# Building a stacked factor operand on chip from eight loaded copies, in a batched low-rank-updated linear layer

## The reference

```python
# x: (32, 512, 512)   fside -> u = v: (32, 1, 512, 16)   cond: (32, 512)   W: (512, 512)   fc_bias: (512,)
z1 = einsum('bfi,bir->bfr', x, v[:, 0]) / 512
z  = einsum('bfr,bor->bfo', z1, u[:, 0]) / 16
y  = einsum('bfi,oi->bfo', x, W) + fc_bias + z + cond[:, None, :]
out = x + gelu(y)                      # exact gelu, float32 throughout
```

## Time and profile before

| | |
|---|---|
| median of three runs | 387.24 us |
| the profiled execution's own time | 387.57 us |
| span of its instructions | 385.8 us (1.8 us lie around it) |
| TensorE (PE) busy | 376.9 us |
| VectorE (DVE) busy | 296.7 us |
| ScalarE (ACT) busy | 204.6 us |
| DMA | 85.75 MB, mean 222 GB/s |

### The profile page before, as it was taken

The page is one execution under the profiler, slowest core; times in us unless marked ns, Lnnn a source line. Parts: engine busy times, 40 slices in busy tenths (PEclk is TensorE's granted clock), DMA queues, the critical chain, the costliest instruction groups (busy, mean ns, idle before and its releaser), DMA issues.

```text
span 385.8 us, 7835 instructions
## 1 busy us (share of the span) xinstructions
PE 376.9 (98%) x3065; PEld 313.8 (81%) x3065; DVE 296.7 (77%) x188; ACT 204.6 (53%) x214; POOL 0.7 (0%) x5
## 2 busy tenths in 40 slices
PE   8998899999999999999999999999999999999995
PEld 3676788888888888888888888888888888888884
DVE  2579967788877878888777897778888787788832
ACT  3467364545566445566545556654465664455531
POOL 0000000000000000000000000000000000000000
PEclk9999899999999999999999999999999999999999
DMA  7879789887777877777787777687767779774222
GB/s 193 229 152 304 220 268 270 265 263 233 213 231 225 261 221 248 211 218 234 239 244 231 244 212 221 213 266 220 256 230 206 230 218 270 216 255 131 110 109 110
DMA packets 27756, 85.75 MB, mean 222 GB/s; under 512 B 6832, under 2 KB 6960, under 8 KB 23776
## 3 DMA queue, kind: packets, MB, share of 16 engines
q1 hardware_dynamic: 27088, 84.41, 71.8%
q10 hardware_dynamic: 656, 1.18, 1.0%
HBM read 35.75 MB, written 33.55 MB: 180 GB/s over the span
## 4 chain that ended last, share of the span: by engine, by line
PE 89%; SPq 5%; DMA 2%; ACTq 1%; ACT 1%; DVE 1%; issue 0%
PE y L420 82%; SPq L178 5%; PE update L489 3%; DMA f_stack<-f_parts 2%; ACTq L274 1%; PE y L404 1%; PE y L412 1%; PE y L408 1%; ACT L279 0%; SPq L164 0%; SPq L192 0%; ACT result L270 0%; DVE result L356 0%; DVE x_low L313 0%; DVE f_parts L313 0%
## 5 line engine op out<-in xcount | busy, mean ns | idle before, releaser
L420 PE MATMUL y<-x_low,w_high 64*128 64x512 f32 x928 | 184.5, 388 | 0.0
L420 PE MATMUL y<-x_high,w_high 64*128 64x512 f32 x928 | 184.5, 388 | 0.0
L270 ACT ACTIVATE result<-y,bias 128x512 f32<-128x512 f32 x128 | 81.4, 685 | 156.9 <-PE y L420 148.6
L420 PE MATMUL y<-x_high,w_low 64*128 64x512 f32 x928 | 125.2, 387 | 0.0
L356 DVE TENSOR_TENSOR result<-result,x_in 128x1024 f32<-128x1024 f32 (+1 forms) x65 | 78.3, 1205 | 56.5 <-ACT result L270 56.5
L420 PEld LDWEIGHTS y<-x_high,w_low 64*128 64x128 f32 x928 | 90.5, 185 | 15.3
L420 PEld LDWEIGHTS y<-x_low,w_high 64*128 64x128 f32 x928 | 90.5, 185 | 15.3
L420 PEld LDWEIGHTS y<-x_high,w_high 64*128 64x128 f32 x928 | 90.3, 185 | 15.3
L317 DVE SCALAR_TENSOR_TENSOR full_w<-update,base_w 128x2048 f32<-128x2048 f32 (+1 forms) x38 | 74.3, 1954 | 23.6 <-PE update L489 16.9
L313 DVE TENSOR_TENSOR x_low<-x_in,x_high 128x2048 fp32r<-128x2048 f32 (+1 forms) x38 | 74.0, 1947 | 5.6 <-ACT x_high L256 5.6
L313 DVE TENSOR_TENSOR w_low<-full_w,w_high 128x2048 fp32r<-128x2048 f32 (+1 forms) x38 | 74.0, 1948 | 0.4
(11 more groups left out here) (15 smaller groups left out, 29.7 us busy)
## 6 DMA issues: line engine op xcount, KB each, us to landing
out_t<-result SPq DMA_DIRECT2D x63, 512.0 KB, 3.1
x_in<-x_t SPq DMA_DIRECT2D x31, 1024.0 KB, 6.5
f_stack<-f_parts SPq DMA_DIRECT2D x186, 64.0 KB, 4.1
f_stack<-f_parts SPq DMA_DIRECT2D x124, 32.0 KB, 3.8
x_in<-x_t ACTq DMA_DIRECT2D x4, 256.0 KB, 9.3
base_w<-w_t SPq DMA_DIRECT2D x4, 256.0 KB, 8.2
f_parts<-factors SPq DMA_DIRECT2D x1, 896.0 KB, 6.8
out_t<-result SPq DMA_DIRECT2D x2, 256.0 KB, 2.5
```

Of the source, the lines that this page charges most:

```text
L270: nc.scalar.activation(result[j % SLOTS][:, m, :], y[m][:, :], ACT.Gelu, bias=bias[:, bass.ds(b * CHUNKS + m, 1)]).then_inc(gelu_ready, 1)
L420: return nc.tensor.matmul(y[m][:, :], w[rows, c, m * P:(m + 1) * P], x[rows, c, :], start=first, stop=last)
```

## The change

The stack is no longer copied together. Each batch's raw factors (16 rows) are loaded from HBM in eight copies into the 128 partitions of `f_raw` by one DMA. ScalarE rounds all 128 rows to `f_high`; VectorE makes each side of the stack as `f_high * low_rows[side] + f_raw`, where `low_rows` is a column with -1 in rows that shall hold the low part and 0 elsewhere. A row with 0 holds the raw factor, which is rounded as it is written in fp32r. The column is made once from row numbers: an iota on GpSimd, two `bitwise_and` and two multiplications on VectorE. `f_raw` has four buffers, `f_high` and `f_stack` two.

`f_first` becomes 128 rows: 16 of factors, 16 of zeros from HBM, 96 zeroed by two VectorE memsets. ScalarE's queue no longer loads factors. SP's first loads come in another order. All four first updates stand ahead of piece 0, and the update of batch 1 moves from ahead of piece 2 to ahead of piece 3, with a wait per chunk. `w_t` and `factors` have other layouts in HBM.

```diff
-    RANK = factors.shape[0] // UNROLL
+    RANK = factors.shape[1]
+    COPIES = P // RANK
-        f_first = sb("f_first", [RANK, FEATURES], fp32)
-        f_parts = sb("f_parts", [UNROLL * RANK, GROUPS, 3, FEATURES], fp32)
+        f_first = sb("f_first", [P, FEATURES], fp32)
+        f_raw = [sb(f"f_raw{s}", [P, FEATURES], fp32) for s in range(UNROLL)]
+        f_high = [sb(f"f_high{s}", [P, FEATURES], fp32r) for s in range(SLOTS)]
...
+        def stacked_in(t, j):
+            return t + (j + 2) // UNROLL, (j + 2) % UNROLL
+        def has_stack(t, j):
+            return not (isinstance(t, int) and t == GROUPS - 1 and j >= UNROLL - 2)
...
         @block.sync
+            def load_factors(t, j):
+                sp.dma_start(f_raw[j][:, :],
+                             factors[bass.ds(UNROLL * t + j, 1)].to_broadcast([COPIES, RANK, FEATURES])
+                             ).then_inc(f_loaded[j], 16)
-            sp.dma_start(f_first[:, :], factors[0:RANK, 0, :]).then_inc(f_first_loaded, 16)
+            sp.dma_start(f_first[0:FIRST_ROWS, :], first_factors).then_inc(f_first_loaded, 16)
             for c in range(CHUNKS):
-                sp.dma_start(base_w[:, c, :], w_t[:, c, :]).then_inc(w_loaded[c], 16)
+                sp.dma_start(base_w[:, c, :], w_t[c]).then_inc(w_loaded[c], 16)
+                if c == 1:
+                    load_factors(0, 1)
             load_x(0, 1)
             sp.dma_start(cond_sb[:, :, :], cond).then_inc(bias_loaded, 16)
             sp.dma_start(fc_sb[:, :], fc_bias).then_inc(bias_loaded, 16)
-            sp.wait_ge(f_low_ready, 1)
-            stack_factors(0, 1)
-            stack_factors(0, 2)
-            sp.dma_start(f_parts[:, 1:GROUPS, 2, :], factors[:, 1:GROUPS, :]).then_inc(f_loaded[1], 16)
-            for j in range(2, X_SLOTS):
-                load_x(0, j)
+            load_factors(0, 2)
+            load_x(0, 2)
+            load_factors(0, 3)
+            load_x(0, 3)
             def step(t, j):
-                if not (last_group and j >= UNROLL - 3):
-                    sp.wait_ge(update_ready, made(b + 1))
-                    stack_factors(t3, j3)
...
                     load_x(t + 1, j)
+                    if not is_first(t, j):
+                        sp.wait_ge(stack_ready, 2 * b)
+                    load_factors(t + 1, j)
...
         @block.scalar
+            def high_factors(t, j):
+                act.wait_ge(f_loaded[j], 16 * (t + 1) if j else 16 * t)
+                if not (isinstance(t, int) and b < SLOTS + 1):
+                    act.wait_ge(stack_ready, 2 * (b - SLOTS))
+                nc.scalar.activation(f_high[j % SLOTS][:, :], f_raw[j][:, :], ACT.Copy).then_inc(f_high_ready, 1)
             for c in range(CHUNKS):
                 high_pieces(0, c)
-                if c == 0:
-                    split_factors(0)
+                if c == 1:
+                    high_factors(0, 1)
             def step(t, j):
...
                     split_x(tn, jn)
                     split_w(tn, jn)
+                    if not piecewise(t, j) and has_stack(t, j):
+                        high_factors(*stacked_in(t, j))
                 for m in range(CHUNKS if is_whole(t, j) else TILES):
                     gelu(t, j, m)
                 if piecewise(tn, jn):
                     for c in range(CHUNKS // 2, CHUNKS):
                         high_pieces(b + 1, c)
-                if j == 0 and not last_group:
-                    split_factors(t + 1)
+                if piecewise(t, j):
+                    high_factors(*stacked_in(t, j))
...
         @block.vector
+            def stack_factors(t, j):
+                if isinstance(t, int) and b == 1:
+                    dve.wait_ge(low_rows_ready, 2)
+                dve.wait_ge(f_high_ready, b)
+                if not (isinstance(t, int) and b < SLOTS + 1):
+                    dve.wait_ge(update_ready, made(b - SLOTS))
+                for side in range(2):
+                    nc.vector.scalar_tensor_tensor(f_stack[slot][:, side, :], f_high[slot][:, :].bitcast(fp32),
+                                                   low_rows[:, side:side + 1], f_raw[j][:, :], ALU.mult,
+                                                   ALU.add).then_inc(stack_ready, 1)
+            nc.vector.memset(f_first[FIRST_ROWS:2 * FIRST_ROWS, :], 0.0).then_inc(f_first_zeroed, 1)
+            nc.vector.memset(f_first[2 * FIRST_ROWS:P, :], 0.0).then_inc(f_first_zeroed, 1)
+            dve.wait_ge(rows_numbered, 1)
+            bits = (2 * RANK, RANK)
+            for side in range(2):
+                nc.vector.tensor_scalar(row_bit[:, side:side + 1], rows[:, :], bits[side], None,
+                                        ALU.bitwise_and).then_inc(bits_ready, 1)
+            dve.wait_ge(bits_ready, 2)
+            for side in range(2):
+                nc.vector.tensor_scalar(low_rows[:, side:side + 1], row_bit[:, side:side + 1], -1.0 / bits[side], None,
+                                        ALU.mult).then_inc(low_rows_ready, 1)
             for c in range(CHUNKS):
                 pieces(0, c)
-                if c == 0:
-                    low_factors(0)
+                if c == 1:
+                    stack_factors(0, 1)
...
-                if j == 1 and not (isinstance(t, int) and t == GROUPS - 1):
-                    low_factors(t + 1)
             def step(t, j):
...
                     low_part(w_low[slot][:, :, :], full_w[:, :, :], w_high[slot][:, :, :], w_low_ready)
+                if has_stack(t, j):
+                    stack_factors(*stacked_in(t, j))
                 if piecewise(t, j):
                     finish_previous(t, j)
                 add_x(t, j, slice(0, HALF))
...
         @block.gpsimd
             nc.gpsimd.memset(idle[:, :], 0.0).then_inc(idle_zeroed, 1)
+            nc.gpsimd.iota(rows[:, :], [[0, 1]], base=0, channel_multiplier=1).then_inc(rows_numbered, 1)
...
         @block.tensor
-                pe.wait_ge(stacked[slot], 16 * STACK_DMAS * uses)
-                pe.wait_ge(full_w_ready, made(b - 1))
+                pe.wait_ge(stack_ready, 2 * b)
+                if not piecewise(t, j):
+                    pe.wait_ge(full_w_ready, made(b - 1))
                 for c in range(CHUNKS):
+                    if piecewise(t, j):
+                        pe.wait_ge(full_w_ready, made(b - 2) + c + 1)
...
+            pe.wait_ge(f_first_zeroed, 2)
             pe.wait_ge(f_first_loaded, 16)
-            for c in range(CHUNKS - 1):
+            for c in range(CHUNKS):
                 first_update(c)
             for c in range(CHUNKS):
-                if c == 1:
-                    first_update(CHUNKS - 1)
-                if c == CHUNKS // 2:
+                if c == CHUNKS - 1:
                     rank_update(0, 1)
                 piece(0, c)
```

More of the change, by code:

```diff
@@ L28, with cond_residual_kernel @@
 UNROLL = 4
-def cond_residual_kernel(nc, x_t, w_t, factors, cond, fc_bias, out_t):
+def cond_residual_kernel(nc, x_t, w_t, first_factors, factors, cond, fc_bias, out_t):
     fp32 = mybir.dt.float32
     fp32r = mybir.dt.float32r
+    int32 = mybir.dt.int32
     ALU = mybir.AluOpType
@@ L39, in cond_residual_kernel @@
     GROUPS = BATCHES // UNROLL
-    RANK = factors.shape[0] // UNROLL
+    RANK = factors.shape[1]
+    FIRST_ROWS = first_factors.shape[0]
+    COPIES = P // RANK
     UPDATE_SCALE = 1.0 / (FEATURES * RANK)
@@ L45, in cond_residual_kernel @@
     TILE = P // TILES
-    STACK_DMAS = 5 * TILES
     HALF = CHUNKS // 2
@@ L90, in cond_residual_kernel @@
         f_first_loaded = sem("f_first_loaded")
-        f_loaded = [sem("f_loaded_group0"), sem("f_loaded_rest")]
+        f_first_zeroed = sem("f_first_zeroed")
+        f_loaded = [sem(f"f_loaded{s}") for s in range(UNROLL)]
+        rows_numbered = sem("rows_numbered")
+        bits_ready = sem("bits_ready")
+        low_rows_ready = sem("low_rows_ready")
         bias_loaded = sem("bias_loaded")
@@ L96, in cond_residual_kernel @@
         f_high_ready = sem("f_high_ready")
-        f_low_ready = sem("f_low_ready")
-        stacked = [sem(f"stacked{s}") for s in range(SLOTS)]
+        stack_ready = sem("stack_ready")
         bias_ready = sem("bias_ready")
@@ L556 @@
     x_t = np.ascontiguousarray(x.transpose(0, 2, 1))
-    w_t = np.ascontiguousarray(np.asarray(L0_cond_W).reshape(P, chunks, P, chunks).transpose(2, 3, 1, 0)
-                               .reshape(P, chunks, features))
-    factors = np.asarray(fside_Bx1x1024x16_0).reshape(batches // UNROLL, UNROLL, P, chunks, rank)
-    factors = np.ascontiguousarray(factors.transpose(1, 4, 0, 3, 2).reshape(UNROLL * rank, batches // UNROLL, features))
+    w_t = np.ascontiguousarray(np.asarray(L0_cond_W).reshape(P, chunks, P, chunks).transpose(3, 2, 1, 0)
+                               .reshape(chunks, P, features))
+    factors = np.asarray(fside_Bx1x1024x16_0).reshape(batches, P, chunks, rank)
+    factors = np.ascontiguousarray(factors.transpose(0, 3, 2, 1).reshape(batches, rank, features))
```

(2 more changed lines are left out.)

33 lines of the change are left out of this document (7 added, 26 removed).

## The result

**Slower by 0.42%.** The changed kernel takes 387.62 us (386.42 to 389.23, 20 runs), the kernel before in the same session 385.87 us (384.55 to 388.07, 20 runs). The ratio is 1.0042, its 95% interval 1.0022 to 1.0061: slower, clear of noise, though the interval's lower end is under the 0.3% that I had taken as the least that can be told. I had forecast 385.9 and given 0.12 to slower. That 387.62 lies inside my range (383.8 to 387.8) is luck: the range reached so far up for a late load at batch 1, which did not come. Note that the kernel before, too, did not come out at the 387.24 of the three runs that I had; that turns out to be part of the error.

The account below looks back on a forecast made before the run. TensorE's back-to-back products bound the kernel, so only the head could gain: -1.4 us from 387.57 gave 386.2, or 385.8 beside the median 387.24; stated 385.9 us. Range 383.8 to 387.8.

Parts of the forecast that it names:

- a late load at batch 1: Batch 1's eight-copy factors landing late; the range's upper end, 387.8 us, assumed landing at 13.6 us with a clock fall.
- the walk through the head: From first updates to batch 3's update, operation times added in the new order: that update at 38.2 us, 1.4 us gained.
- the signs that I had named for being wrong: ScalarE awaiting f_raw past 13 us, VectorE starting past 6.5, batch period above 11.33, or a third TensorE wait in the head.
- the rival: Batch 1's eight-copy load uses only some DMA engines, lands at 12.4 to 15 us: 386.5 to 389.1 us; chance 0.14.
- From batch 3 on the pace is 11.33 in both.: Steady state from batch 3: each batch takes 11.33 us before and after the change, so nothing gained or lost.
- whether VectorE's load fits: Steady state: two added stack operations, 1.37 us, bring VectorE to 10.4 us of each 11.33 us batch, costing nothing.
- Update 3 starts at 38.2 in place of 39.64: 1.4 us gained: Head: batch 3's update, released by VectorE's stack instead of a transfer, starts 1.4 us earlier, at 38.2 us.
- The sum: Whole kernel: head gain of 1.4 us, the clock's fall costing 1.65 us both before and after, steady pace unchanged.
- Its loads wait for a stack made two batches earlier: nothing.: Steady state, SP's queue: factor loads wait only for a stack made two batches earlier, so they cost nothing.
- The stall leaves the clock alone: Rival at the wait before batch 3's update: no clock fall, gain 1.4 + 1.65 = 3.05 us, 384.2 us; chance 0.27.

Follow-up runs that it names:

- second profile of the kernel before: The kernel before, unedited, run and profiled again: 385.27 us, ratio 0.9987; the clock did not fall in this profile.
- the filled wait with the loads first: Changed kernel with small tiles declared last, eight-copy loads at the start of SP's step, and 14 zero products before batch 3's update: 385.28 us, ratio 0.9981.
- second profile of the changed kernel: The changed kernel, unedited, run and profiled again: 387.59 us, ratio 1.0046 to the kernel before.
- the kernel with the wait filled: Changed kernel with 14 products of zeros on TensorE ahead of batch 3's update, nothing else: 387.27 us, ratio 1.0029 to the kernel before.

## Why the prediction was wrong, point by point

**Right: the walk through the head.** The factors of batch 1 are rounded at 11.20 (I had 11.7), update 1 is at 17.71 (17.7), gelu is the next thing late (0.89 at 22.31), update 2 at 29.12 (28.8), the wait ahead of update 3 is 3.15 us (3.3) and ends at 38.68 (38.2), the clock falls again and costs again 12.54 - 10.90 = 1.64 (1.65). The iota takes 0.13 us at 1.29. VectorE has 10.38 us a batch (10.4). That last one is right with one size off: a stack operation takes 747 ns and not 0.69 us.

Of the signs that I had named for being wrong one came, and it is the first failed step below: a batch period above 11.33.

**The load of eight copies.** At 210 us, when the packets on their way are those of the factors' load (98 packets, 0.20 MB in that microsecond, 2 KB each), the DMA share is 0.51 and 195 GB/s move; at 205 us it is 1.03 and 410. Half of the engines' time, then, and half of the rate, as in the rival. The rule of the Trainium skill, DMA: Bandwidth & Descriptors, Rules for kernel authors, agrees with this trace. But ScalarE had the first load at 11.20 us, after 0.46 us of waiting for it and 0.5 before my 11.7, so the rival's cost for batch 1 was not there. It came back in a place that I didn't look at, the factors of batch 4.

**The failed steps** are four.

1. *"From batch 3 on the pace is 11.33 in both."* It is 11.367: 0.033 x 27 = 0.90 us. I had asked for this step whether VectorE's load fits, and it does; with half of it gone the pace stays. The cost came in with three declarations. Shown from both sides: the small tiles moved last take it away, an unused tile of the same size puts 0.027 of it into the kernel before. Against the execution of the earlier trace rows this alone turns 0.93 us of gain into nothing, hence the equal spans.

2. *"Update 3 starts at 38.2 in place of 39.64: 1.4 us gained."* The head gained 0.93 us against that execution, as stack 3 came 0.5 us later than in the walk (its rounding 0.3 late, the two stack operations 1.41 in place of 1.3). That is the mis-sized term. Worse is the base: 39.64 is update 3 in one execution. In the second profile of the kernel before it is at 38.79, and with the unused tiles at 38.35 to 39.67. The term of 1.4 us is 0.1 against the second profile, and 39.64 is near the late end of all six.

3. *The sum was made against an execution of the less frequent kind, and the clock's fall cancelled in it.* I set one fall against one fall. But 38 of 103 runs of the kernel before have a mean clock of 0.996 or less, and 23 of 32 of the changed kernel. That a fall costs 1.6 us where the stack comes no earlier is shown by the filled wait with the loads first. That the longer wait is why it comes more often is supported by the profiles kept. The clock fell behind waits of TensorE for a stack of 1.92, 2.21, 2.24, 2.93, 3.12 (twice), 3.15 and 3.17 us; it stayed up behind all thirteen of 0.41 to 1.61 us, and behind one of 2.93 us, in the second profile of the changed kernel. The wait ahead of update 3 is 1.16 to 2.24 us in the six executions with the head of the kernel before, by how late the stack's transfers land, and 2.93 to 3.17 in the five with the head of the changed one that don't fill it. The frequencies themselves are of runs without a trace, so their cause is not shown run by run. The wait of 0.9 us for gelu, which only the changed kernel has, brings the clock down now and then: in two of the ten profiles that have it.

4. *"Its loads wait for a stack made two batches earlier: nothing."* The load of batch 4 waits for more than that: it stands in SP's queue behind a store and a load of x, issued at 40.65, and ScalarE stands 3.8 us for it. Where the clock falls at update 3 the slow piece covers it; where it doesn't, TensorE waits for stack 4, 0.68 us in the second profile and 0.42 in the kernel with the wait filled. With its wait filled the changed kernel so got only 0.8 of the 1.6 us of a fall, and the rest with the loads first.

**The sum again**, with what was measured: +0.9 for the pace. For the head, batch 3's products start at 53.35 with a fall and 50.89 without in the kernel before, at 52.42 with a fall and 51.63 without in the changed one (the last from the kernel with the wait filled). Weighted with how often the clock falls, 38 of 103 and 23 of 32, this is 51.8 against 52.2, +0.4, an estimate from four executions; +1.3 in all. The ratio of 1.0042 is 1.6 us with an interval of 0.8 to 2.4. Runs with two falls, probably the five with a mean clock of 0.990, are not in the sum. By these starts a run of the changed kernel without a fall is 51.63 - 50.89 + 0.90 = 1.6 us slower than one of the kernel before without a fall, and the runs show 1.7. Two chains compared directly, before without and after with a fall, give by parts: batch 3's products start at 52.42 against 50.89, 1.53 later (1.62 for the clock, -0.11 for update 3, 0.02 for the update), and the last piece at 359.32 against 356.89, 2.43 later, 0.90 more.

**Why none of my rivals was it.** The rival on the other side was the late load; its mechanism is there, its price at batch 1 was not. "The stall leaves the clock alone" had the right doubt, from the spread of three times over 1.3 us, but I read it as a chance for the changed kernel alone. The same spread said that the base moves.

**Open.** Why the place of f_stack in SBUF, or of the small tiles behind it, which the experiments moved along, changes the time of the update and of the five pairs of products behind it. The weight loads' busy time is no lead: it is 37.35 with the unused tile of 32 bytes and 37.41 in the second profile of the changed kernel, both at the slow pace, and 38.80 in the kernel before. And what decides whether a wait of a given length brings the clock down in a given run. None was tried further.

## What to carry to other kernels

A profile is one execution: where TensorE waits for some microseconds, look first at the mean granted clock of all runs, and make the sum against the frequent kind, since a change can move how often the clock falls. Here declaring the small new tiles behind the large ones took a loss away, which costs nothing to try in another kernel; and compare the pace per batch to the hundredth of a microsecond over many batches: 0.033 us is invisible in any one instruction and was the largest term here. When a late step is made early, follow its input back to the issue of the load before saying what it brings, for the wait only moves if the next thing on that path is as late. The same goes for a stall that is taken away: here a second one stood behind it, half as long.

## What was not expected of the hardware

- An unused tile of 16, 20 or 32 bytes a partition ahead of f_stack lengthened a batch from 11.333 to 11.360 us, one of 64 bytes to 11.387.
- A scalar_tensor_tensor with a column as its scalar took 747 ns at 128x512, against 0.69 us for the one without a column that reads PSUM; which of the differences between them costs it was not tried.
- First updates of 128 rows, most of them zeros, let the products behind them run at the fast pace (four in 1.07 us at 10.70); behind 16-row ones four took 1.91 us at 10.85 in the kernel before. The recorded granted clock was 1.00 in both.
- Fourteen products of zeros in a wait of 3.1 us kept the clock up behind it, in the two profiles taken; 6 of the 24 runs still have a mean clock of 0.996 or less.
